# v behind the second half of the scores, and the next image's statistics beside the first scores, in an attention kernel

## The chip, the cores and the metric

The kernel runs on one NeuronCore of a Trainium2 chip. The metric is the device time of one execution in microseconds. The kernel before took 1803.81 us, the median of three runs (1803.52 to 1804.42).

## What is computed

The input x has 32 images of 32 x 32 positions with 256 channels. Each image is normalised by groups (32 groups of 8 channels, over all positions), goes through single-head self-attention over its 1024 positions, and is added to x:

```python
scale = jnp.float32(c) ** (-0.5)
x = inputs.reshape(B, H * W, c)
q = x @ Wq + bq
k = x @ Wk + bk
v = x @ Wv + bv
scores = jnp.einsum('bnc,bmc->bnm', q, k) * scale
attn = jax.nn.softmax(scores, axis=-1)
attended = jnp.einsum('bnm,bmc->bnc', attn, v)
out = attended @ Wo + bo
...
x = x + _L0_conv_ref(_gn(x), ...)
```

## The kernel before

Wq and Wk are folded into one matrix, Wv and Wo into another, so that each image needs one projection "g" (4 banks of 128 x 512), one projection "v" (4 banks), the scores of h with g, and the attend of the exponentials with v. Every float32 operand of a matmul is kept as a coarse part (`_hi`) and a rest (`_lo`), and a product is three matmuls (hi hi, hi lo, lo hi).

An image b is worked in two halves c of 512 queries. The scores of a half are 8 tiles m (128 keys x 512 queries, 6 matmuls each, `scores`, L933). They go through four PSUM banks `ps_s`; ScalarE reads each out to `s_buf[c]` (`scores_out`, L343), and TensorE may write tile m + 4 only then (semaphore `s_out`). VectorE takes the maximum over the 8 tiles (`maxima`, five steps, L584), turns and reduces it (`part_maxima`, `query_maxima`, `row_maxima`), and subtracts it in four pieces of two tiles (`difference`, L621). ScalarE makes two exponentials of each piece: the coarse `p_hi` (`exponentials_hi`, L349) and the full one in place (`exponentials`, L358); VectorE makes the rest `p_lo` (`p_rest`, L628). The attend (L946) is four tiles j of 24 matmuls into `ps_o[j]`; its first tile waits for `p_lo` piece by piece. `finish` (L636) divides by the sum of the exponentials (a column of ones in v) and adds the bias; POOL's `store` adds the result to a copy of x in the output.

The banks of g and v are shared with these: `ps_g` is `ps_o[0]`, `ps_o[1]`, `ps_s[2]`, `ps_s[3]`. ScalarE reads g and v out (`g_part`, `v_part`), VectorE makes their rests (`g_rest`, `v_rest`).

The next image is prepared beside this. SP loads x_t(b + 1) as soon as `h_rest(b)` is done. VectorE takes its statistics (`channel_stats`, `channel_sums`, `group_means`, `group_spread`, `group_variance`), POOL raises to the power -1/2 (`inverse_std`), VectorE turns the result back (`turn_back`), ScalarE shifts x_t in place (`shift`) and makes `h_hi` (`h_parts`), VectorE `h_lo` (`h_rest`), and TensorE projects g(b + 1).

Nothing schedules this: each engine has a list written out by hand, and takes its instructions in that order. TensorE's (L995) is, per image:

```python
for m in range(T):
    scores(b, 0, m)
for j in range(TQ):
    attend(b - 1, 1, j)
project_v(b, first=first)
for m in range(T):
    scores(b, 1, m, first_v=first)
for j in range(TQ):
    attend(b, 0, j)
project_g(b + 1)
```

Image 0 has lists of its own (`first_image`), the last one too (`last_image`); images 1 to 30 take `body`. In image 1 VectorE's `body(1, True)` puts the statistics behind the last `v_rest` (late_stats), in the others they stand ahead of the first.

Of the kernel before, what the change touches and what calls it, by code (L numbers as in the profile page):

```python
# [42 lines left out]
def attention_kernel(nc, x, x_turned, wq, bq, wk, bk, wv, bv, wo, bo, out):  # L43
    B, H, W, C = x.shape
    N = H * W
    T = N // P
# [6 lines left out]
    NP = T // PIECE  # L53
# [13 lines left out]
    with ExitStack() as ctx:  # L67
# [103 lines left out]
        bn_done = sem("bn_done")  # L171
# [105 lines left out]
        @block.gpsimd  # L277
        def _(pool):
            pool.memset(ident[:], 0.0).then_inc(const_step, 1)
            pool.memset(chan[:], 0.0).then_inc(const_step, 1)  # L280
            pool.memset(ones[:], 1.0).then_inc(const_step, 1)
            pool.memset(minus_half[:], -0.5).then_inc(const_step, 1)
            pool.memset(v_hi[:, :, 0:1].bitcast(F32), 1.0).then_inc(const_step, 1)
            pool.memset(v_hi[:, :, 1:VC - C].bitcast(F32), 0.0).then_inc(const_step, 1)
            pool.wait_ge(const_step, 6)
            pool.affine_select(out=ident[:], in_=ident[:], compare_op=ALU.not_equal, fill=1.0, base=0,
                               pattern=[[-1, P]], channel_multiplier=1).then_inc(const_step, 1)

            def store(b, c):

                after(pool, x_copied[c], b * 16 + 16)
                after(pool, o_out, b * 8 + (4 * c + 4))
                pool.dma_start(out_v[b, :, c * TQ:(c + 1) * TQ, :], o_buf[c][:],  # L293
                               accum_op=ALU.add).then_inc(stored[c], 16)

            def inverse_std(b):
                pool.wait_ge(var_done, b + 1)
                pool.tensor_tensor(group_stats[:, 1, :], g_var[:], minus_half[:], ALU.pow).then_inc(rstd_done, 1)  # L298

            inverse_std(0)  # L300

            inverse_std(1)
            store(0, 0)
            with pool.Fori(1, B - 1) as b:
                store(b - 1, 1)
                inverse_std(b + 1)
                store(b, 0)
            store(B - 2, 1)
            store(B - 1, 0)
# [3 lines left out]
        def _(act):  # L313
# [4 lines left out]

            def h_parts(b):
                act.wait_ge(s_ps, b * 16)  # L320
                for k in range(K):
                    act.wait_ge(h_done, b * 2 + (k + 1))
                    nc.scalar.activation(h_hi[:, k, :], x_t[:, k, :], ACT.Identity,
                                         scale=norm[:, 1, k:k + 1]).then_inc(h_hi_done, 1)
# [24 lines left out]
            def exponentials_hi(b, c, i):  # L349

                rows = slice(i * PIECE, (i + 1) * PIECE)
                if i == 0:
                    after(act, o_ps, b * 8 + (4 * c + 4 - 8))
                act.wait_ge(diff_done, b * 8 + (4 * c + i + 1))
                nc.scalar.activation(p_hi[c][:, rows, :], s_buf[c][:, rows, :], ACT.Exp,  # L355
                                     scale=SCALE).then_inc(p_hi_done, 1)
# [33 lines left out]
            act.wait_ge(fold_ps, 4)  # L390
            nc.scalar.activation(out_bias[:], ps_ob[:, 0:C], ACT.Copy).then_inc(out_bias_done, 1)

            def softmax_beside(b, c, project):

                for i in range(NP - 1):
                    exponentials_hi(b, c, i)
                    if i == 1:
                        project(2)
                    exponentials(b, c, i)
                    if i == 0:  # L400
                        project(0)
                        project(1)
                    elif i == 1:
                        project(3)

            def last_exponentials(b, c):
                exponentials_hi(b, c, NP - 1)
                exponentials(b, c, NP - 1)

            def first_image():  # L410

# [36 lines left out]
                for m in range(4, T):  # L448
                    scores_out(1, 0, m)

            def scores_first(b):

                scores_out(b, 0, 0)
                last_exponentials(b - 1, 1)
                for m in range(1, T):
                    scores_out(b, 0, m)

            def body(b):

                softmax_beside(b, 0, lambda i: v_part(b, i))  # L460
                scores_out(b, 1, 0)
                last_exponentials(b, 0)
                for m in range(1, T):
                    scores_out(b, 1, m)
                shift(b + 1, 0)
                shift(b + 1, 1)
                h_parts(b + 1)
                softmax_beside(b, 1, lambda i: g_part(b + 1, i))

            def last_image(b):  # L470

                scores_out(b, 0, 0)
                last_exponentials(b - 1, 1)
                for m in range(1, T):
                    scores_out(b, 0, m)
                scores_out(b, 1, 0)
                scores_out(b, 1, 1)
                scores_out(b, 1, 2)
                for i in range(NP):
                    exponentials_hi(b, 0, i)  # L480
                    exponentials(b, 0, i)
                    scores_out(b, 1, 3 + i)
                scores_out(b, 1, 7)
                for i in range(4):
                    v_part(b, i)
                for i in range(NP):
                    exponentials_hi(b, 1, i)
                    exponentials(b, 1, i)
# [1 line left out]
            first_image()  # L490
            body(1)
            with act.Fori(2, B - 1) as b:
                scores_first(b)
                body(b)
            last_image(B - 1)

# [2 lines left out]
        def _(dve):  # L499
# [195 lines left out]
            def first_image():  # L695
# [45 lines left out]
                p_rest(0, 1, 1)  # L741
                finish(0, 0, 3)
                p_rest(0, 1, 2)
                maxima(1, 0, 0)
                p_rest(0, 1, 3)
                for step in range(1, 5):
                    maxima(1, 0, step)

            def softmax_beside(b, c, finish_tile, h_next, project, next_stats, next_sums, late_stats=False):

                part_maxima(b, c)
                finish_tile(0)
                h_next(0)
                h_next(1)
                query_maxima(b, c)
                finish_tile(1)
                row_maxima(b, c)
                difference(b, c, 0)
                difference(b, c, 1)
                finish_tile(2)  # L760
                difference(b, c, 2)
                if not late_stats:
                    next_stats()
                project(0)
                if not late_stats:
                    next_sums()
                finish_tile(3)
                project(1)
                p_rest(b, c, 0)
                project(2)  # L770
                difference(b, c, 3)
                project(3)
                if late_stats:
                    next_stats()
                p_rest(b, c, 1)
                if late_stats:
                    next_sums()
                p_rest(b, c, 2)
                p_rest(b, c, 3)

            def scores_first(b):

                for step in range(5):
                    maxima(b, 0, step)

            def body(b, late_stats=False):
                def next_stats():
                    channel_stats(b + 1)
                    dve.wait_ge(bn_done, b * 4 + 8)

                softmax_beside(b, 0, lambda j: finish(b - 1, 1, j), nothing, lambda i: v_rest(b, i),
                               next_stats, lambda: channel_sums(b + 1), late_stats)
                group_means(b + 1)
                group_spread(b + 1)
                maxima(b, 1, 0)
                group_variance(b + 1)
                maxima(b, 1, 1)
                maxima(b, 1, 2)
                turn_back(b + 1)
                maxima(b, 1, 3)  # L800
                maxima(b, 1, 4)
                softmax_beside(b, 1, lambda j: finish(b, 0, j), lambda k: h_rest(b + 1, k),
                               lambda i: g_rest(b + 1, i), nothing, nothing)

            def last_image(b):

# [40 lines left out]
                                        ALU.add).then_inc(x_last_done, 1)  # L847

            first_image()
            body(1, True)  # L850
            with dve.Fori(2, B - 1) as b:
                scores_first(b)
                body(b)
# [7 lines left out]
        def _(pe):  # L861
# [52 lines left out]
                    product(ps_g[i][:], [(a[:, kk, rows], h[:, kk, cols]) for kk in range(K)  # L914
                                             for a, h in ((a_hi, h_hi), (a_hi, h_lo), (a_lo, h_hi))], g_ps)

            def project_v(b, scores_done=8, first=False):

                for i in FIRST_V if first else range(4):
                    if first and i >= 2:  # L920
# [74 lines left out]
            def body(b, first=False):  # L995
                for m in range(T):
                    scores(b, 0, m)
                if not first:
                    for j in range(TQ):
                        attend(b - 1, 1, j)  # L1000
                project_v(b, first=first)
                for m in range(T):
                    scores(b, 1, m, first_v=first)
                for j in range(TQ):
                    attend(b, 0, j)
                project_g(b + 1)

            def last_image(b):
# [47 lines left out]
```

## Time and profile before

| | |
|---|---|
| median of 3 runs | 1803.81 us (1803.52 to 1804.42) |
| the profiled execution, its own time | 1804.24 us |
| its span in the profile | 1802.6 us |
| granted TensorE clock | 1.00 throughout |
| TensorE busy | 1796.6 us (100%) |
| VectorE busy | 1638.7 us (91%) |
| ScalarE busy | 1056.1 us (59%) |
| GpSimd (POOL) busy | 91.1 us (5%) |

Times in the timelines are microseconds from the start of the span; the execution's own time is 1.6 us more than the span. Matmuls are pipelined and overlap in the records, each lasting 0.28 or 0.39 us while they follow one another more closely, so the length of a stage is read from start to start. A row of a timeline that ends in x2 or x4 is a run of like instructions, and its length that of the whole run.

### The profile page before, as it was taken

The page shows a single profiled execution, that of the slowest core. Times are in us where ns is not written, and L with a number is a line of the kernel's source. Part 1 is how long each engine was busy: PE and PEld are TensorE (multiplying, and loading weights), DVE is VectorE, ACT ScalarE, POOL GpSimd, SP SyncE. Part 2 cuts the span into 40 slices and gives each one's busy share as a digit, 9 for nine tenths or more (in the row PEclk, how much of TensorE's full clock was granted, in tenths as well). Part 3 has the DMA queues.
Part 4 walks back from the last instruction along what each step waited for, and adds up shares of the span by engine and source line. Part 5 has one row for each costly group of instructions (what it writes and reads, how often), then busy time and mean ns, then how long its engine had stood idle before and what let it go on. Part 6 is the DMA issues. An engine that isn't in the chain of part 4 may idle for free.

```text
span 1802.6 us, 32710 instructions
## 1 busy us (share of the span) xinstructions
PE 1796.6 (100%) x11589; PEld 1643.1 (91%) x11589; DVE 1638.7 (91%) x2860; ACT 1056.1 (59%) x1417; POOL 91.1 (5%) x106
## 2 busy tenths in 40 slices
PE   9999999999999999999999999999999999999999
PEld 8989999899899999998999989999899898999989
DVE  7999899999999999989999999899998999999997
ACT  5565565665655656556565565565665656656563
POOL 0000000000000000000000000000000000000000
PEclk9999999999999999999999999999999999999999
DMA  3222122321222221213212222122321222311201
GB/s 117 59 71 69 26 57 58 70 70 37 44 60 68 70 54 27 70 58 70 58 23 70 58 70 65 23 64 58 70 70 36 46 60 68 70 48 33 67 14 36
DMA packets 28809, 101.92 MB, mean 57 GB/s; under 512 B 3189, under 2 KB 3962, under 8 KB 28794
## 3 DMA queue, kind: packets, MB, share of 16 engines
q0 software_dynamic: 9072, 33.03, 12.1%
q1 hardware_dynamic: 19722, 68.69, 11.7%
q8 instruction: 9, 0.15, 0.0%
q14 instruction: 6, 0.05, 0.0%
HBM read 68.16 MB, written 66.58 MB: 75 GB/s over the span
## 4 chain that ended last, share of the span: by engine, by line
PE 97%; DVE 2%; issue 1%; POOL 0%; ACT 0%; POOLq 0%; DVEq 0%; ACTq 0%
PE ps_s L865 48%; PE ps_o L959 13%; PE ps_o L960 13%; PE ps_o L961 13%; PE ps_o L865 10%; DVE s_buf L625 0%; PE ps_o L969 0%; DVE top L595 0%; DVE o_buf L645 0%; DVE h_lo L567 0%; DVE query_max L612 0%; POOL group_stats L298 0%; DVE top_turned L600 0%; DVE g_lo L575 0%; DVE part_max L602 0%
## 5 line engine op out<-in xcount | busy, mean ns | idle before, releaser
L959 PE MATMUL ps_o<-v_rows,p_hi 128*128 128x258 f32 x2048 | 577.9, 282 | 0.0
L961 PE MATMUL ps_o<-v_rows,p_lo 128*128 128x258 f32 x2048 | 576.1, 281 | 0.0
L960 PE MATMUL ps_o<-v_lo,p_hi 128*128 128x256 f32 x2048 | 575.8, 281 | 0.0
L355 ACT ACTIVATE p_hi<-s_buf 128x1024 fp32r<-128x1024 f32 x256 | 272.3, 1063 | 417.6 <-DVE s_buf L625 417.6
L865 PE MATMUL ps_s<-g_hi,h_hi 128*128 128x512 f32 x1024 | 399.2, 390 | 0.4 <-DVE g_lo L575 0.3
L865 PE MATMUL ps_s<-g_hi,h_lo 128*128 128x512 f32 x1024 | 399.0, 390 | 0.0
L865 PE MATMUL ps_s<-g_lo,h_hi 128*128 128x512 f32 x1024 | 398.6, 389 | 0.0
L959 PEld LDWEIGHTS ps_o<-v_rows,p_hi 128*128 128x128 f32 x2048 | 385.9, 188 | 2.4
L960 PEld LDWEIGHTS ps_o<-v_lo,p_hi 128*128 128x128 f32 x2048 | 384.8, 188 | 2.9
L347 ACT ACTIVATE s_buf<-ps_s 128x512 f32<-128x512 f32 x512 | 293.1, 607 | 160.4 <-PE ps_s L865 158.7
L961 PEld LDWEIGHTS ps_o<-v_rows,p_lo 128*128 128x128 f32 x2048 | 384.5, 188 | 0.0
L633 DVE TENSOR_TENSOR p_lo<-s_buf,p_hi 128x1024 fp32r<-128x1024 f32 x256 | 306.9, 1219 | 39.1 <-ACT s_buf L361 39.1
L625 DVE TENSOR_TENSOR s_buf<-s_buf,row_max 128x1024 f32<-128x1024 f32 x256 | 306.7, 1219 | 2.1
L361 ACT ACTIVATE s_buf<-s_buf 128x1024 f32<-128x1024 f32 x256 | 271.3, 1060 | 0.0
L865 PEld LDWEIGHTS ps_s<-g_hi,h_hi 128*128 128x128 f32 x1024 | 192.2, 188 | 40.4 <-issue 0.8
L865 PEld LDWEIGHTS ps_s<-g_hi,h_lo 128*128 128x128 f32 x1024 | 192.2, 188 | 40.3
L865 PEld LDWEIGHTS ps_s<-g_lo,h_hi 128*128 128x128 f32 x1024 | 192.2, 188 | 38.8
L595 DVE TENSOR_TENSOR top<-top,s_buf 128x512 f32<-128x512 f32 (+1 forms) x192 | 167.3, 871 | 40.1 <-ACT s_buf L347 25.0
L645 DVE SCALAR_TENSOR_TENSOR o_buf<-ps_o,rden,out_bias 128x256 f32<-128x256 f32 x252 | 121.9, 484 | 14.5
L293 POOL DMA_DIRECT2D out_dram<-o_buf x63 | 56.1, 891 | 1397.5 <-DVE o_buf L645 1380.2
L340 ACT ACTIVATE v_rows<-ps_o 128x512 fp32r<-128x512 f32 x64 | 38.3, 599 | 105.9 <-PE ps_o L865 105.8
L595 DVE TENSOR_TENSOR top<-s_buf 128x1024 f32<-128x1024 f32 x64 | 78.2, 1222 | 7.7 <-ACT s_buf L347 7.7
(95 smaller groups left out, 2229.6 us busy)
## 6 DMA issues: line engine op xcount, KB each, us to landing
x_t<-in_x_turned_dram SPq DMA_DIRECT2D x64, 512.0 KB, 4.0
out_dram<-in_x_dram SPq DMA_DIRECT2D x63, 512.0 KB, 7.1
out_dram<-o_buf POOLq DMA_DIRECT2D x63, 512.0 KB, 5.4
x_last<-in_x_dram SPq DMA_DIRECT2D x1, 512.0 KB, 7.8
out_dram<-o_buf SPq DMA_DIRECT2D x4, 128.0 KB, 1.9
s_buf<-in_L_conv_Wq_dram SPq DMA_DIRECT2D x1, 256.0 KB, 4.6
s_buf<-in_L_conv_Wk_dram SPq DMA_DIRECT2D x1, 256.0 KB, 5.0
s_buf<-in_L_conv_Wv_dram SPq DMA_DIRECT2D x1, 256.0 KB, 5.2
```

The costliest lines, as they stand in the source:

```text
L293: pool.dma_start(out_v[b, :, c * TQ:(c + 1) * TQ, :], o_buf[c][:], accum_op=ALU.add).then_inc(stored[c], 16)
L347: nc.scalar.activation(s_buf[c][:, m, :], ps_s[(8 * c + m) % SB][:], ACT.Copy).then_inc(s_out, 1)
L355: nc.scalar.activation(p_hi[c][:, rows, :], s_buf[c][:, rows, :], ACT.Exp, scale=SCALE).then_inc(p_hi_done, 1)
L361: nc.scalar.activation(piece, piece, ACT.Exp, scale=SCALE).then_inc(p_done, 1)
L595: nc.vector.tensor_tensor(to, left, right, ALU.max).then_inc(top_step, 1)
L625: nc.vector.tensor_tensor(piece, piece, row_max[:].unsqueeze(1).broadcast_to([P, PIECE, Q]), ALU.subtract).then_inc(diff_done, 1)
L633: nc.vector.tensor_tensor(p_lo[c][:, rows, :], s_buf[c][:, rows, :], p_hi[c][:, rows, :].bitcast(F32), ALU.subtract).then_inc(p_lo_done, 1)
L645: nc.vector.scalar_tensor_tensor(out=o_buf[c][:, j, :], in0=ps_o[j][:, VC - C:VC], scalar=rden[:, t:t + 1], in1=out_bias[:] if rows is Non ...
L865: last = nc.tensor.matmul(ps, stationary, moving, start=start and n == 0, stop=stop and n == len(pairs) - 1)
L959: nc.tensor.matmul(ps[:, 0:VC], p_hi[c][:, m, cols], v_hi[:, m, :], start=m == 0, stop=False)
L960: nc.tensor.matmul(ps[:, VC - C:VC], p_hi[c][:, m, cols], v_lo[:, m, :], start=False, stop=False)
L961: last = nc.tensor.matmul(ps[:, 0:VC], p_lo[c][:, m, cols], v_hi[:, m, :], start=False, stop=m == T - 1)
```

## The change

TensorE takes `project_v(b)` behind the second half of the scores, right ahead of `attend(b, 0)`. The scores of the second half no longer wait for `v_lo`; v's third bank waits for the readout of all 16 score tiles instead of 8; `attend(b, 0)` waits for `v_lo` by piece in its first tile. Image 0 keeps the old order. ScalarE and VectorE get new lists for the body to match, for image 1 too (no late_stats), and the last pair of exponentials of c = 1 is done within the image. VectorE's statistics of image b + 1 stand beside the maxima of the first scores of b. POOL takes `inverse_std(b + 1)` ahead of `store(b - 1, 1)`.

```diff
             with pool.Fori(1, B - 1) as b:
+                inverse_std(b + 1)
                 store(b - 1, 1)
-                inverse_std(b + 1)
                 store(b, 0)
...
             def h_parts(b):
                 act.wait_ge(s_ps, b * 16)
+                act.wait_ge(v_ps, b * 4)
                 for k in range(K):
...
+            def pair(b, c, i):
+                exponentials_hi(b, c, i)
+                exponentials(b, c, i)
...
             def body(b):
                 shift(b + 1, 0)
                 shift(b + 1, 1)
+                pair(b, 0, 0)
+                pair(b, 0, 1)
+                scores_out(b, 1, 0)
+                pair(b, 0, 2)
+                scores_out(b, 1, 1)
+                scores_out(b, 1, 2)
+                exponentials_hi(b, 0, 3)
+                scores_out(b, 1, 3)
+                exponentials(b, 0, 3)
+                for m in range(4, T):
+                    scores_out(b, 1, m)
+                for i in range(4):
+                    v_part(b, i)
                 h_parts(b + 1)
+                pair(b, 1, 0)
+                pair(b, 1, 1)
+                g_part(b + 1, 0)
+                exponentials_hi(b, 1, 2)
+                g_part(b + 1, 1)
+                exponentials(b, 1, 2)
+                g_part(b + 1, 2)
+                exponentials_hi(b, 1, 3)
+                g_part(b + 1, 3)
+                exponentials(b, 1, 3)
             def last_image(b):
+                for m in range(T):
                     scores_out(b, 0, m)
                 scores_out(b, 1, 0)
                 scores_out(b, 1, 1)
...
             first_image()
             body(1)
             with act.Fori(2, B - 1) as b:
-                scores_first(b)
+                for m in range(T):
+                    scores_out(b, 0, m)
                 body(b)
             last_image(B - 1)
...
                 p_rest(0, 1, 1)
                 finish(0, 0, 3)
                 p_rest(0, 1, 2)
                 p_rest(0, 1, 3)
+                scores_first(1)
             def scores_first(b):
+                channel_stats(b + 1)
+                dve.wait_ge(bn_done, b * 4 + 8)
+                maxima(b, 0, 0)
+                channel_sums(b + 1)
+                maxima(b, 0, 1)
                 group_means(b + 1)
                 group_spread(b + 1)
+                maxima(b, 0, 2)
                 group_variance(b + 1)
+                maxima(b, 0, 3)
+                maxima(b, 0, 4)
+            def body(b):
+                part_maxima(b, 0)
                 turn_back(b + 1)
+                finish(b - 1, 1, 0)
+                query_maxima(b, 0)
+                finish(b - 1, 1, 1)
+                row_maxima(b, 0)
+                difference(b, 0, 0)
+                difference(b, 0, 1)
+                finish(b - 1, 1, 2)
+                difference(b, 0, 2)
+                difference(b, 0, 3)
+                finish(b - 1, 1, 3)
+                for i in range(NP):
+                    p_rest(b, 0, i)
+                for step in range(5):
+                    maxima(b, 1, step)
+                v_rest(b, 0)
+                part_maxima(b, 1)
+                for i in (1, 2, 3):
+                    v_rest(b, i)
+                query_maxima(b, 1)
+                row_maxima(b, 1)
+                h_rest(b + 1, 0)
+                h_rest(b + 1, 1)
+                finish(b, 0, 0)
+                difference(b, 1, 0)
+                difference(b, 1, 1)
+                finish(b, 0, 1)
+                difference(b, 1, 2)
+                difference(b, 1, 3)
+                finish(b, 0, 2)
+                finish(b, 0, 3)
+                g_rest(b + 1, 0)
+                g_rest(b + 1, 1)
+                p_rest(b, 1, 0)
+                g_rest(b + 1, 2)
+                p_rest(b, 1, 1)
+                g_rest(b + 1, 3)
+                p_rest(b, 1, 2)
+                p_rest(b, 1, 3)
             def last_image(b):
...
                                         ALU.add).then_inc(x_last_done, 1)
             first_image()
-            body(1, True)
+            body(1)
             with dve.Fori(2, B - 1) as b:
                 scores_first(b)
                 body(b)
...
                     product(ps_g[i][:], [(a[:, kk, rows], h[:, kk, cols]) for kk in range(K)
                                              for a, h in ((a_hi, h_hi), (a_hi, h_lo), (a_lo, h_hi))], g_ps)
-            def project_v(b, scores_done=8, first=False):
+            def project_v(b, scores_done=16, first=False):
                 for i in FIRST_V if first else range(4):
                     if first and i >= 2:
...
                 if not first:
                     for j in range(TQ):
                         attend(b - 1, 1, j)
-                project_v(b, first=first)
-                for m in range(T):
-                    scores(b, 1, m, first_v=first)
+                if first:
+                    project_v(b, first=True)
+                    for m in range(T):
+                        scores(b, 1, m, first_v=True)
+                else:
+                    for m in range(T):
+                        scores(b, 1, m, True)
+                    project_v(b, 16)
                 for j in range(TQ):
-                    attend(b, 0, j)
+                    attend(b, 0, j, not first)
                 project_g(b + 1)
             def last_image(b):
```

The new lists are shown with "+"; the old ones that they replace stand in the listing above. Below, the rows of three places as they stand on the engine (line, operation, tiles, shape). The changed kernel's lines are three lower on VectorE and one higher on most of ScalarE's.

VectorE, from the third `p_rest` of image 0 on (`p_lo` is written by `p_rest`, `top` by `maxima`, `top_turned` by `part_maxima`), before:

```order
L633 TENSOR_TENSOR p_lo<-s_buf,p_hi 128x1024
L595 TENSOR_TENSOR top<-s_buf 128x1024
L633 TENSOR_TENSOR p_lo<-s_buf,p_hi 128x1024
L595 TENSOR_TENSOR top<-top,s_buf 128x1024
L595 TENSOR_TENSOR top<-top 128x512
L595 TENSOR_TENSOR top<-top,s_buf 128x512 x2
L600 STREAM_TRANSPOSE top_turned<-top 128x512
L602 TENSOR_REDUCE part_max<-top_turned 128x16
L640 RECIPROCAL rden<-ps_o 128x1
L645 SCALAR_TENSOR_TENSOR o_buf<-ps_o,rden,out_bias 128x256
L609 COPY parts<-part_max 32x16 x4
```

And in the changed kernel:

```order
L630 TENSOR_TENSOR p_lo<-s_buf,p_hi 128x1024 x2
L502 BN_STATS bn_parts<-x_t 128x6 x4
L592 TENSOR_TENSOR top<-s_buf 128x1024
L508 BN_AGGR chan<-bn_parts 128x2 x2
L592 TENSOR_TENSOR top<-top,s_buf 128x1024
L519 STREAM_TRANSPOSE chan_turned<-chan 128x64
L522 TENSOR_REDUCE mean_sum<-chan_turned 128x4
L527 SCALAR_TENSOR_TENSOR dev<-mean_sum,chan_turned 128x32
L530 TENSOR_SCALAR group_stats<-mean_sum 128x4
L533 TENSOR_TENSOR dev<-dev 128x32
L535 TENSOR_TENSOR spread<-chan_turned,dev 128x32
L592 TENSOR_TENSOR top<-top 128x512
```

The statistics of image 2, from `bn_parts` to `spread`, have come in ahead of the maxima and between them, and the last `p_rest` of image 0 stands ahead of all of them.

ScalarE, in image 1 from the end of the first half's readouts on (`s_buf<-ps_s` is a readout of a score, `v_rows` one of v, `p_hi<-s_buf` and `s_buf<-s_buf` are the two exponentials of a piece), before:

```order
L355 ACTIVATE p_hi<-s_buf 128x1024
L361 ACTIVATE s_buf<-s_buf 128x1024
L340 ACTIVATE v_rows<-ps_o 128x2x256 x2
L355 ACTIVATE p_hi<-s_buf 128x1024
L340 ACTIVATE v_rows<-ps_s 128x2x256
L361 ACTIVATE s_buf<-s_buf 128x1024
L340 ACTIVATE v_rows<-ps_s 128x2x256
L355 ACTIVATE p_hi<-s_buf 128x1024
L361 ACTIVATE s_buf<-s_buf 128x1024
L347 ACTIVATE s_buf<-ps_s 128x512
L355 ACTIVATE p_hi<-s_buf 128x1024
L361 ACTIVATE s_buf<-s_buf 128x1024
```

And in the changed kernel:

```order
L317 ACTIVATE x_t<-x_t,norm 128x1024 x2
L356 ACTIVATE p_hi<-s_buf 128x1024
L362 ACTIVATE s_buf<-s_buf 128x1024
L356 ACTIVATE p_hi<-s_buf 128x1024
L362 ACTIVATE s_buf<-s_buf 128x1024
L348 ACTIVATE s_buf<-ps_s 128x512
L356 ACTIVATE p_hi<-s_buf 128x1024
L362 ACTIVATE s_buf<-s_buf 128x1024
L348 ACTIVATE s_buf<-ps_s 128x512 x2
L356 ACTIVATE p_hi<-s_buf 128x1024
L348 ACTIVATE s_buf<-ps_s 128x512
L362 ACTIVATE s_buf<-s_buf 128x1024
```

The shift (`x_t`) leads, the readouts of v have left the exponentials, and the first readout of the second half stands behind four exponentials instead of six and the four of v.

VectorE, in image 1 from the first `p_rest` of the first half on, before:

```order
L633 TENSOR_TENSOR p_lo<-s_buf,p_hi 128x1024
L581 TENSOR_TENSOR v_lo<-ps_s,v_rows 128x512
L625 TENSOR_TENSOR s_buf<-s_buf,row_max 128x1024
L581 TENSOR_TENSOR v_lo<-ps_s,v_rows 128x512
L505 BN_STATS bn_parts<-x_t 128x6 x4
L633 TENSOR_TENSOR p_lo<-s_buf,p_hi 128x1024
L511 BN_AGGR chan<-bn_parts 128x2 x2
L633 TENSOR_TENSOR p_lo<-s_buf,p_hi 128x1024 x2
```

And in the changed kernel:

```order
L630 TENSOR_TENSOR p_lo<-s_buf,p_hi 128x1024 x4
L592 TENSOR_TENSOR top<-s_buf 128x1024
L592 TENSOR_TENSOR top<-top,s_buf 128x1024
L592 TENSOR_TENSOR top<-top 128x512
L592 TENSOR_TENSOR top<-top,s_buf 128x512 x2
L578 TENSOR_TENSOR v_lo<-ps_o,v_rows 128x512
L597 STREAM_TRANSPOSE top_turned<-top 128x512
L599 TENSOR_REDUCE part_max<-top_turned 128x16
L578 TENSOR_TENSOR v_lo<-ps_o,v_rows 128x512
L578 TENSOR_TENSOR v_lo<-ps_s,v_rows 128x512 x2
L606 COPY parts<-part_max 32x16 x4
```

`v_rest` (`v_lo`) has moved from between the `p_rest` to behind the maxima of the second half, the first one ahead of the transpose and reduction, the other three behind them.

## Rows read from the trace of the kernel before

**Rows 1.** The page's busy times by engine, over the whole span
```profile
PE 1796.6 (100%) x11589; PEld 1643.1 (91%) x11589; DVE 1638.7 (91%) x2860; ACT 1056.1 (59%) x1417; POOL 91.1 (5%) x106
```

**Rows 2.** The page's costly groups: first matmuls of a score (busy, mean, idle before)
```profile
L865 PE MATMUL ps_s<-g_hi,h_hi 128*128 128x512 f32 x1024 | 399.2, 390 | 0.4 <-DVE g_lo L575 0.3
```

**Rows 3.** Timeline of TensorE, image 16: start us, length, engine, line, instruction
```profile
901.44 0.39 PE L865 MATMUL ps_s<-g_hi,h_hi 128*128 128x512 f32 x1
...
923.76 0.28 PE L865 MATMUL ps_o<-vo_hi,h_hi 128*128 128x256 f32 x1
...
929.36 0.40 PE L865 MATMUL ps_s<-g_hi,h_hi 128*128 128x512 f32 x1
...
940.27 0.28 PE L959 MATMUL ps_o<-v_rows,p_hi 128*128 128x258 f32 x1
...
957.16 0.39 PE L865 MATMUL ps_s<-g_hi,h_hi 128*128 128x512 f32 x1
```

**Rows 4.** Timeline of ScalarE, image 1 (idle before it in brackets)
```profile
86.78 1.06 ACT L355 ACTIVATE p_hi<-s_buf 128x1024 fp32r<-128x1024 f32 x1 [10.05 <-DVE s_buf L625]
...
94.60 1.06 ACT L361 ACTIVATE s_buf<-s_buf 128x1024 f32<-128x1024 f32 x1
95.55 0.60 ACT L347 ACTIVATE s_buf<-ps_s 128x512 f32<-128x512 f32 x1
96.03 1.08 ACT L355 ACTIVATE p_hi<-s_buf 128x1024 fp32r<-128x1024 f32 x1
```

**Rows 5.** The page's DMA issues (KB each, us from issue to landing)
```profile
x_t<-in_x_turned_dram SPq DMA_DIRECT2D x64, 512.0 KB, 4.0
```

**Rows 6.** Timeline of VectorE, image 1
```profile
85.46 2.36 DVE L625 TENSOR_TENSOR s_buf<-s_buf,row_max 128x1024 f32<-128x1024 f32 x2
...
94.42 0.68 DVE L581 TENSOR_TENSOR v_lo<-ps_s,v_rows 128x512 fp32r<-128x512 f32 x1
95.02 2.46 DVE L505 BATCH_NORM_STATS2 bn_parts<-x_t 128x6 f32<-128x512 f32 x4
...
98.66 0.28 DVE L511 BATCH_NORM_AGGREGATE chan<-bn_parts 128x2 f32<-128x12 f32 x2
98.85 2.31 DVE L633 TENSOR_TENSOR p_lo<-s_buf,p_hi 128x1024 fp32r<-128x1024 f32 x2
101.08 0.24 DVE L522 STREAM_TRANSPOSE chan_turned<-chan 128x64 f32<-128x64 f32 x1
...
102.13 1.22 DVE L595 TENSOR_TENSOR top<-s_buf 128x1024 f32<-128x1024 f32 x1
103.26 0.18 DVE L543 TENSOR_REDUCE var_sum<-spread 128x4 f32<-128x32 f32 x1
...
103.56 1.23 DVE L595 TENSOR_TENSOR top<-top,s_buf 128x1024 f32<-128x1024 f32 x1
...
105.78 0.24 DVE L550 STREAM_TRANSPOSE norm<-group_stats 128x64 f32<-128x64 f32 x1 [0.27 <-POOL group_stats L298]
105.95 1.38 DVE L595 TENSOR_TENSOR top<-top,s_buf 128x512 f32<-128x512 f32 x2
107.36 0.71 DVE L600 STREAM_TRANSPOSE top_turned<-top 128x512 f32<-128x512 f32 x1
...
108.72 0.16 DVE L640 RECIPROCAL rden<-ps_o 128x1 f32<-128x1 f32 x1
```

**Rows 7.** Timeline of TensorE, image 1, first matmul of v
```profile
87.31 0.28 PE L865 MATMUL ps_o<-vo_hi,h_hi 128*128 128x256 f32 x1
```

**Rows 8.** Timeline of TensorE, from image 1 to image 2
```profile
120.48 0.39 PE L865 MATMUL ps_s<-h_hi,a_lo 128*128 128x512 f32 x1
121.22 0.49 PE L865 MATMUL ps_s<-g_hi,h_hi 128*128 128x512 f32 x1 [0.35 <-DVE g_lo L575]
121.55 0.40 PE L865 MATMUL ps_s<-g_lo,h_hi 128*128 128x512 f32 x1
```

**Rows 9.** Windows: length, busy (x), granted clock, DMA share, GB/s, first microseconds
```profile
2.00:8.00 6.00, 5.99 (x32) 5.99 (x33) 3.44 (x10) 0.15 (x1) 0.00 (x0) 1.00 0.96 343
```

More of the change, by code:

```diff
@@ L391, in _ @@
             nc.scalar.activation(out_bias[:], ps_ob[:, 0:C], ACT.Copy).then_inc(out_bias_done, 1)
[L393 to L408, printed above, removed]
+            def pair(b, c, i):
+                exponentials_hi(b, c, i)
+                exponentials(b, c, i)
             def first_image():
@@ L449, in first_image @@
                     scores_out(1, 0, m)
[L451 to L456, printed above, removed]
-            def body(b):
[L460 to L464, printed above, removed]
+            def body(b):
                 shift(b + 1, 0)
                 shift(b + 1, 1)
-                h_parts(b + 1)
-                softmax_beside(b, 1, lambda i: g_part(b + 1, i))
+                pair(b, 0, 0)
[11 more added lines that the diff above has]
+                    v_part(b, i)
+                h_parts(b + 1)
+                pair(b, 1, 0)
[8 more added lines that the diff above has]
+                exponentials(b, 1, 3)
             def last_image(b):
-                scores_out(b, 0, 0)
-                last_exponentials(b - 1, 1)
-                for m in range(1, T):
+                for m in range(T):
                     scores_out(b, 0, m)
@@ L743, in first_image @@
                 p_rest(0, 1, 2)
-                maxima(1, 0, 0)
                 p_rest(0, 1, 3)
[L746 to L779, printed above, removed]
@@ L781, in scores_first @@
-            def scores_first(b):
[L783 to L792, printed above, removed]
+                scores_first(1)
@@ L793, in body @@
+            def scores_first(b):
+                channel_stats(b + 1)
[3 more added lines that the diff above has]
+                maxima(b, 0, 1)
                 group_means(b + 1)
                 group_spread(b + 1)
-                maxima(b, 1, 0)
+                maxima(b, 0, 2)
                 group_variance(b + 1)
-                maxima(b, 1, 1)
-                maxima(b, 1, 2)
+                maxima(b, 0, 3)
+                maxima(b, 0, 4)
@@ L799, in body @@
+            def body(b):
+                part_maxima(b, 0)
                 turn_back(b + 1)
[L800 to L803, printed above, removed]
+                finish(b - 1, 1, 0)
[36 more added lines that the diff above has]
+                p_rest(b, 1, 3)
```

## Prediction

> **What bounds the kernel now.** I read the busy times first, then TensorE's waits, then the timeline of a middle image, then that of image 1, since the change handles image 1 like the rest where the old code had an exception for it. TensorE is busy throughout and VectorE 91% [rows 1]; the 1024 first matmuls of the score groups lost 0.4 us in all to waits [rows 2]. The middle image [rows 3] has no hole: first half of the scores, attend of the image before (c=1), v, second half of the scores, attend (c=0), projection of g. The starts give the stage lengths: v 929.36 - 923.76 = 5.60, a half of the scores 940.27 - 929.36 = 10.91, so an attend 923.76 - 901.44 - 10.91 = 11.41, g 957.16 - 940.27 - 11.41 = 5.48, the image 957.16 - 901.44 = 55.72 us. The 32 images at that pace are 1783 of 1802.6 us; the rest is set-up and the tail. So the same matmuls cannot go faster than they go. **An edit of the order can win only the few tenths that TensorE waits, and can lose where it makes TensorE wait.** The sum is a count of new holes on TensorE.
>
> **The change part by part.** No instruction is added or removed but for waits. I give times from the start of an image's first score ("t"); ScalarE's and VectorE's steps are start-to-start intervals.
>
> *TensorE.* Second half of the scores now starts at 10.91 + 11.41 = 22.32, where v stood, v at 33.23, attend c=0 at 38.83 as before. Sum of the stages: unchanged. The scores lose their wait on v_lo; v's third bank waits for the readout of the last score; the first tile of attend waits for v_lo by piece, 0.72 us apart (a tile is 11.41 / 4 = 2.85, a piece a quarter of it).
>
> *ScalarE and VectorE in a middle image.* ScalarE now puts the four readouts of g between the last two pairs of exponentials instead of carrying the last pair into the next image. The first g bank is ready at -5.48 + 1.37 + 0.2 = -3.9; four more exponentials at 0.95 (95.55 - 94.60 [rows 4]) and three readouts, by my estimate 0.57 each, put the last exponential's end at about 2.3. VectorE follows with p_rest 2 and 3 and begins the statistics of the next image at about 4.9. What stands between there and the first difference is priced on image 1 next; carried over, the first readout of the second half ends at about 25.0, while TensorE needs it for the fifth score at 22.32 + 5.46 = 27.8: 2.8 spare. The last exponential of c=0 ends at 30.2; then p_rest 1.12, five maxima 4.75, v_rest 0 to 36.7, transpose and reduction 1.36, v_rest 1 to 38.7, needed at 38.83 + 0.72 = 39.55: 0.85 spare. v_rest 3 hangs on TensorE's own pace: v ends 38.83, readout from 39.05 to 39.65, v_rest to 40.35, needed at 41.0: 0.65 spare, the thinnest joint, and VectorE idles some tenths ahead of it. h_lo is done at about 45.3, needed at 50.2. g_lo 1 is done some 0.8 ahead of the next image's first score. **So the middle images cost nothing: 0.**
>
> *Moved statistics and the queues.* The load of x_t is issued when h_lo is done, at t of about 45, and lands 4.0 us later [rows 5]; the statistics, which used to read it half an image later, now read it some 15 us behind the issue. Still covered; if the cover were gone, VectorE would wait there with the maxima behind it and TensorE behind those. On POOL the inverse deviation now stands ahead of the store of the image before; its input is ready at t of about 12, the store's not before 24, so the store is not delayed. The shift on ScalarE (two steps of about 1.1) falls into the wait ahead of the first exponential, 10 us long in image 1 [rows 4]. h_hi now waits for v too, which ends at 38.83, as the readouts ahead of it do. Each of these: 0.
>
> *Image 1.* It comes from first_image, whose order is the old one, so here the lead is missing. In the trace the first difference of image 1 starts at 85.46 [rows 6]. Ahead of it the change now puts the statistics of image 2, which the old code had (late_stats) behind the v_rests: bn_stats 2.46; channel sums 98.85 - 98.66 = 0.19; group means and spread 102.13 - 101.08 = 1.05; variance 103.56 - 103.26 = 0.30; turn_back 105.95 - 105.78 = 0.17; together 4.17 [rows 6]. Difference 0 starts at 89.63. The second half of the scores starts where v did, at 87.31 [rows 7], 5.60 us earlier than it did: **4.2 us later meets 5.6 us earlier.** In steps:
> - ScalarE starts the first exponential 86.78 - 85.46 = 1.32 behind difference 0 [rows 4, 6]: 90.95. The readout of score 0 stands behind four exponentials, 0.95 each: 94.75, ends after 0.60 at 95.35.
> - TensorE wants its bank for the fifth score at 87.31 + 5.46 = 92.77. Hole of 2.58, 0.05 for the signal.
> - Readout 1 stands behind one more readout and two exponentials: 94.75 + 0.48 (96.03 - 95.55 [rows 4]) + 1.90 = 97.13, ends 97.73. TensorE, due at 95.40 + 0.10 + 1.36 = 96.86, waits to 97.78. (0.10: the first matmul behind a wait takes 0.33 to the next where 0.23 is usual [rows 8].) Readouts 2 and 3 end at 98.2 and 99.6, the latter needed at 100.6. Lost so far: 97.78 - (87.31 + 6.82) = 3.65, with the resumption 3.75.
> - The last exponential runs 99.52 to 100.58; p_rest 3 1.12 (half of 101.08 - 98.85); the maxima 107.36 - 102.13 = 5.23, less 0.30, 0.17 and a wait of 0.27 between them, and some 0.25 more where those steps had filled gaps, 4.75; v_rest 0 0.60 (95.02 - 94.42); transpose and reduction 108.72 - 107.36 = 1.36; v_rest 1 ends 0.68 on, at 109.1 [rows 6]. TensorE ends the scores at 87.31 + 10.91 + 3.75 = 101.97 and wants it at 101.97 + 5.60 + 0.72 = 108.3: 0.8, and 0.1.
> - Statistics now fill gaps between maxima that depend on each other, 0.1 to 0.2 back. Sum about 4.6.
>
> *Given back.* In the old order image 2 opens with a hole: 121.22 - 120.48 = 0.74 between matmuls that are 0.227 apart, and 0.10 behind it [rows 8], since late_stats delayed g_lo. Now g_lo 1 comes some 0.9 before it is needed: -0.6.
>
> **Sum:** 4.6 - 0.6 = +4.0 us on the profiled execution's own 1804.24, which is 0.43 above the median; on the median 1803.81 + 4.0 = **1807.8**. The steps' errors are tenths, those of two medians too: 1807.2 to 1808.6. A measurement of this kernel tells about 0.2%, 3.6 us, from no change; 4.0 is just above.
>
> **Rivals.**
> *A. Not slower: image 1 hides the lateness.* The old ScalarE waited 10 us at this very place [rows 4], and TensorE lost nothing. The deciding point is the readout of score 0: if it ends before 92.77, both score holes go, the later v hole with them (its chain starts with the same exponentials), and the old 0.6 goes too: 1803.81 - 0.6 = 1803.2. For it speaks that wait; against it, that v's 5.60 us lay between it and the scores. 8%.
> *B. Holes in every middle image.* If VectorE is late by over 0.65 to 0.85 us at the v_rests, each further tenth costs 29 x 0.1 = 2.9 us. For it: VectorE has 9% idle and the chain readout, exponential, p_lo, maxima, v_lo stands in one row. At 0.3 us an image: 1807.8 + 8.7 = 1816.5. Against it: the durations repeat within hundredths, and the wait ahead of v_rest 3 is a cushion. 10%.
> *C. The clock falls.* The granted clock was 1.00 in the 6 us behind the first 2 us without a matmul [rows 9]; the new longest hole is 2.6 us, longer than any the trace shows inside the work. If the clock fell to 1.2 GHz for one stage of scores, that costs between nothing and 10.91 again: up to 1818.7. I take nothing, the value of the nearest row. 4%. The Trainium skill (TensorE: Matmul & The Clock Gate, Part 1) says that the array's default is the half rate and that an idle array returns to it. By that rule the pause would be punished twice; the row of this trace doesn't show it.
> *D. Nothing of it bites, or something is gained beyond the 0.6:* 2%; TensorE leaves no room for it.
>
> **How the numbers follow.** Forecast 76%, A 8%, B 10%, C 4%, D 2%. The forecast lies 0.4 above the bound of 3.6 us with an error of that size, so about 7 in 10 of it is slower by over 0.2% and the rest within: slower 0.54 + 0.10 + 0.04 = 0.68; within 0.22 + 0.08 = 0.30; faster 0.02. The range runs from 1805.5 to 1811.5: the forecast with twice its errors, and the mild end of B (0.1 us an image). A and most of B and C, under 2 in 10, stay out.
>
> **What would show it.** In the new profile: TensorE's period in the middle images still 55.72 with no hole; in image 1 two waits for the readouts of scores 0 and 1 of 2.5 and 0.9 us, and one of 0.8 on v_lo in the first attend tile; no wait at the start of image 2; ScalarE's last exponential before the image's first readout; clock 1.00. Wrong would be a period over 55.8, a hole on g_lo or at attend's fourth piece in each image, or image 1 without holes.

## The result, and the profile after

The changed kernel takes 1806.96 us (median of 20 runs, 1806.20 to 1807.77), the kernel before 1804.01 (20 runs). The ratio is 1.0016, 95% interval 1.0010 to 1.0022: 2.95 us more. The forecast was +4.0 and 1807.8. The profiled execution took 1807.02 us, with a span of 1805.3 (before 1802.6).

The page of the changed kernel: busy times, the chain that ended last, and the two groups of TensorE that waited (those of before are [rows 1, 2]).

```profile
PE 1796.1 (99%) x11589; PEld 1641.9 (91%) x11589; DVE 1627.7 (90%) x2860; ACT 1070.1 (59%) x1417; POOL 104.8 (6%) x106
...
PE 95%; DVE 3%; ACT 1%; issue 0%; DMA 0%; SPq 0%; DVEq 0%; ACTq 0%
...
L956 PE MATMUL ps_o<-v_rows,p_hi 128*128 128x258 f32 x2048 | 577.7, 282 | 0.6 <-DVE v_lo L578 0.6
...
L862 PE MATMUL ps_s<-g_hi,h_hi 128*128 128x512 f32 x1024 | 399.2, 390 | 3.1 <-ACT s_buf L348 3.0
```

TensorE did the same work and waited 3.1 us at scores and 0.6 at the attend. The timeline of TensorE shows where: nearly all of it is in image 1 (start us, length, engine, line, instruction).

```profile
87.19 0.40 PE L862 MATMUL ps_s<-g_hi,h_hi 128*128 128x512 f32 x1
...
92.42 0.39 PE L862 MATMUL ps_s<-g_hi,h_lo 128*128 128x512 f32 x1
95.11 0.50 PE L862 MATMUL ps_s<-g_hi,h_hi 128*128 128x512 f32 x1 [2.31 <-ACT s_buf L348]
...
96.38 0.39 PE L862 MATMUL ps_s<-g_hi,h_lo 128*128 128x512 f32 x1
97.50 0.50 PE L862 MATMUL ps_s<-g_hi,h_hi 128*128 128x512 f32 x1 [0.73 <-ACT s_buf L348]
...
101.72 0.28 PE L862 MATMUL ps_o<-vo_hi,h_hi 128*128 128x256 f32 x1
...
107.33 0.28 PE L956 MATMUL ps_o<-v_rows,p_hi 128*128 128x258 f32 x1
...
108.83 0.36 PE L956 MATMUL ps_o<-v_rows,p_hi 128*128 128x258 f32 x1 [0.62 <-DVE v_lo L578]
...
119.62 0.40 PE L862 MATMUL ps_o<-h_hi,a_hi 128*128 128x512 f32 x1
...
125.07 0.39 PE L862 MATMUL ps_s<-g_hi,h_hi 128*128 128x512 f32 x1
```

The second scores took 101.72 - 87.19 = 14.53 us (10.91 before), the attend of the first half ("first attend" below) 119.62 - 107.33 = 12.29 (11.44 before). The idle times in brackets are counted from the modelled end of the matmul ahead. From start to start the three matmuls came 95.11 - 92.42 - 0.23 = 2.46, 0.89 and 0.79 us late. Behind them image 2 starts without a wait, where it had lost 0.6 [rows 8]. The releasers in image 1, first the timeline of ScalarE, then that of VectorE:

```profile
90.68 1.06 ACT L356 ACTIVATE p_hi<-s_buf 128x1024 fp32r<-128x1024 f32 x1 [2.93 <-DVE s_buf L622]
...
94.48 0.58 ACT L348 ACTIVATE s_buf<-ps_s 128x512 f32<-128x512 f32 x1
```

```profile
89.36 2.36 DVE L622 TENSOR_TENSOR s_buf<-s_buf,row_max 128x1024 f32<-128x1024 f32 x2
...
108.00 0.68 DVE L578 TENSOR_TENSOR v_lo<-ps_o,v_rows 128x512 fp32r<-128x512 f32 x1
```

Difference 0 at 89.36 (forecast 89.63), the first exponential at 90.68 (90.95), readout 0 at 94.48 (94.75), v_rest 1 ended at 108.68 (109.1).

The middle images have no wait. In image 16 of the changed kernel, its first score, its difference 0 and its v_rest 1 (timelines of TensorE and VectorE):

```profile
904.68 0.39 PE L862 MATMUL ps_s<-g_hi,h_hi 128*128 128x512 f32 x1
...
923.90 2.36 DVE L622 TENSOR_TENSOR s_buf<-s_buf,row_max 128x1024 f32<-128x1024 f32 x2
...
942.75 0.68 DVE L578 TENSOR_TENSOR v_lo<-ps_o,v_rows 128x512 fp32r<-128x512 f32 x1
```

Difference 0 starts 19.22 us behind the first score there, and 89.36 - 64.87 = 24.49 in image 1: 5.3 later. v_rest 1 ends at 38.75, 0.8 ahead of its need. The first score of image 3 and of image 31 from TensorE's timeline, first in the changed kernel, then in the one before:

```profile
180.76 0.39 PE L862 MATMUL ps_s<-g_hi,h_hi 128*128 128x512 f32 x1
...
1739.98 0.39 PE L862 MATMUL ps_s<-g_hi,h_hi 128*128 128x512 f32 x1
```

```profile
177.08 0.39 PE L865 MATMUL ps_s<-g_hi,h_hi 128*128 128x512 f32 x1
...
1737.24 0.39 PE L865 MATMUL ps_s<-g_hi,h_hi 128*128 128x512 f32 x1
```

28 images take 1559.22 us after and 1560.16 before, 55.686 and 55.720 each: the new order is 0.034 us shorter per image, which the prediction does not have.

### The profile page after: what moved, and what is told of

Read it like the earlier page. It is cut to its first block, busy times and chain, and to the rows that moved or that the text cites. A ratio compares the mean times of both kernels' runs of the same rounds, so it can differ in the third digit from the quotient of the medians.

```text
span 1805.3 us, 32859 instructions
## 1 busy us (share of the span) xinstructions
PE 1796.1 (99%) x11589; PEld 1641.9 (91%) x11589; DVE 1627.7 (90%) x2860; ACT 1070.1 (59%) x1417; POOL 104.8 (6%) x106
## 4 chain that ended last, share of the span: by engine, by line
PE 95%; DVE 3%; ACT 1%; issue 0%; DMA 0%; SPq 0%; DVEq 0%; ACTq 0%
PE ps_s L862 46%; PE ps_o L956 13%; PE ps_o L957 13%; PE ps_o L958 13%; PE ps_o L862 9%; DVE top L592 1%; ACT p_hi L356 0%; ACT s_buf L362 0%; DVE s_buf L622 0%; DMA s_buf<-in_L_conv_Wq_dram 0%; DVE p_lo L630 0%; ACT s_buf L348 0%; DVE o_buf L642 0%; DVE query_max L609 0%; DVE top_turned L597 0%
## 5 line engine op out<-in xcount | busy, mean ns | idle before, releaser
L348 ACT ACTIVATE s_buf<-ps_s 128x512 f32<-128x512 f32 x512 | 301.6, 598 | 196.1 <-PE ps_s L862 190.2
L622 DVE TENSOR_TENSOR s_buf<-s_buf,row_max 128x1024 f32<-128x1024 f32 x256 | 301.6, 1219 | 1.1
L317 ACT ACTIVATE x_t<-x_t,norm 128x1024 f32<-128x1024 f32 x62 | 68.0, 1145 | 117.1 <-DVE norm L547 117.1
```

The lines of the kernel that those rows point to most:

```text
L317: nc.scalar.activation(x_t[:, k, :], x_t[:, k, :], ACT.Identity, bias=norm[:, 0, k:k + 1]).then_inc(h_done, 1)
L348: nc.scalar.activation(s_buf[c][:, m, :], ps_s[(8 * c + m) % SB][:], ACT.Copy).then_inc(s_out, 1)
L622: nc.vector.tensor_tensor(piece, piece, row_max[:].unsqueeze(1).broadcast_to([P, PIECE, Q]), ALU.subtract).then_inc(diff_done, 1)
```

## Experiments

The theory: TensorE's holes are made where VectorE enters the new lists, in image 1, 5.3 us later than in a middle image; elsewhere the order is free. I compare spans of image 1, from its first score to image 2's: before 121.22 - 64.99 = 56.23 us, after 125.07 - 64.87 = 60.20. (Its own start varies by 1.2 us, 64.26 to 65.44, between kernels whose TensorE list is the same up to there, and the whole span varies with it. Runs 2, 3, 4 and 6 are one execution each.)

**1. The old lists in image 1.**

```diff
-            body(1)
+            old_body(1)
+            body(2)
```

`old_body` is the loop body of the kernel before, on TensorE, ScalarE and VectorE; POOL's store of image 0 goes back ahead of the inverse deviation of image 2, and the loops of the new order begin at image 2 or 3.

> All four engines take the old lists in image 1 and the new ones from image 2 on; nothing is left out. Lead theory (TensorE's holes come only from image 1, where VectorE enters the new list some 5.7 us later than in a middle image): the stage of the second scores and the first attend of image 1 go back to 10.9 and 11.4 us, which gives back 3.6 + 0.9 = 4.5; the old hole at the start of image 2 (0.6) returns, and the handover leaves VectorE some 2 us late in image 2, worth one hole of about 1.2 at v_lo there. Span 1802.6 to 1803.0, time about 1804.3. Rival 1 (the new order costs in the middle images and image 1 is incidental): time stays at 1807. Rival 2 (the handover only moves the lateness whole into image 2): again 3.5 to 4.5 of holes, in image 2, time 1806.5 to 1807.5.

Measured 1804.67 us (11 runs; before 1804.25; ratio 1.0002, 0.9993 to 1.0011). Image 1 took 56.23, the old 0.6 is back at image 2, and one hole stands in image 2's first attend (12.56 instead of 11.42). TensorE's waits on v_lo and g_lo in this kernel (total, times, longest):

```profile
PE ps_o L1042 <- DVE v_lo L611: 0.9, 1, 0.9
PE ps_s L948 <- DVE g_lo L605: 0.3, 1, 0.3
```

The lead theory holds: the loss was image 1's, 60.20 - 56.23 = 3.97 us, and of its lateness 1.14 came back in image 2, not the whole.

**2. Fewer statistics in image 1.**

```diff
+            def few_stats(b):
...
+                    nc.vector.bn_stats(bn_parts[:, k, h, :], x_t[:, k, h * Q:h * Q + 16]).then_inc(bn_done, 1)
...
-                scores_first(1)
+                scores_first(1, few_stats)
```

> The changed kernel, but the statistics of image 2 alone are taken over 16 instead of 512 columns per instruction (four bn_stats on VectorE in image 1), so image 2's normalisation is of a sample: work is left out. Lead theory: these instructions shrink from 2.46 to about 0.4 us, everything behind them on VectorE and ScalarE comes 2.0 earlier, the second scores of image 1 take 12.5 instead of 14.53 us, the first attend stays at 12.3 since both the v_rest and TensorE come earlier by the same, span 1803.3. Rival (the holes are made by the order on ScalarE, four exponentials ahead of the first readout, whenever they start, or by the shift ahead of them): both stages stay as they are, span 1805.3.

One run: 1804.29 us, span 1802.6 (1803.3 expected; image 1 began 0.6 earlier than in the changed kernel). The second scores took 12.45 us, the first attend 12.27; image 1 took 58.10, 2.1 less than in the changed kernel. TensorE's waits on engines in this kernel:

```profile
PE ps_s L869 <- ACT s_buf L348: 1.0, 2, 0.7
PE ps_o L963 <- DVE v_lo L585: 0.6, 1, 0.6
```

The hole at the scores shrank by 14.53 - 12.45 = 2.08 us when VectorE had some 2 us less to do ahead of its first difference: it is VectorE's lateness. The wait on v_lo stayed at 0.6.

**3. The statistics alone, v where it was.**

```diff
             def scores_first(b):
+                channel_stats(b + 1)
...
+                maxima(b, 0, 0)
+                channel_sums(b + 1)
...
-            body(1, True)
+            body(1)
```

> The kernel before with one part of the change: the statistics of the next image stand beside the first scores' maxima, in image 1 too; v stays ahead of the second scores, and shift, turn_back and POOL stay where they were. Lead theory: middle images have no hole, period 55.72, since v's 5.6 us still lie between the first half and the readouts of the second. In image 1 the first difference comes 4.1 late; holes of about 1.6 at v_lo in the third score and up to 0.5 more, 2.0 in all, the old 0.6 at image 2 stays or shrinks: span 1804.0 to 1804.8. Rival (the early statistics by themselves cause all of the loss): span 1805.3 or more with 4.5 us of holes in image 1.

One run: 1804.74 us, span 1803.1 (1804.0 to 1804.8 expected; image 1 began 0.7 earlier than in the kernel before). Image 1 took 57.58, 1.35 more than before. TensorE lost 1.86 us in it where 2.0 were expected: 1.36 at v_lo in the third score, the rest at a readout behind it and in v; and no hole is left at image 2. Middle images: (1737.74 - 177.59) / 28 = 55.72. So the early statistics alone cause less than half of image 1's holes. TensorE's wait on v_lo there:

```profile
PE ps_s L869 <- DVE v_lo L581: 1.1, 1, 1.1
```

**4. v alone, the statistics where they were.**

```diff
-                channel_stats(b + 1)
...
                 difference(b, 0, 2)
+                channel_stats(b + 1)
...
                 difference(b, 0, 3)
```

> The changed kernel with the statistics back where the old lists had them (bn_stats behind the third difference, the small steps beside the second half's maxima, the shift ahead of h_hi), v moved as in the change. Lead theory: image 1 has no hole at the scores, but now every image is late at v_lo: the statistics lie between the first difference and v_rest, 2.5 + 1.9 us with an idle of 1.8 to fill, so v_rest 1 ends some 0.9 behind the second piece's due time, 1.0 with the resumption. Period 56.7, 30 images: time 1830 to 1840. Rival (the statistics' place does not matter in the middle images, only v's does): period 55.69, time about 1803 to 1804.

One run: 1830.49 us, span 1828.8. Images 2 to 30 have one hole each, at the second piece of the first attend (12.26 to 12.28 us instead of 11.42), and images 3 to 30 take 56.53 each (56.7 expected). Image 1 has two, of 1.34 us at the first piece and 1.04 at the second, and takes 58.59, more than in the kernel before; but its scores have no hole (10.89). TensorE's waits on v_lo (total, times, longest):

```profile
PE ps_o L958 <- DVE v_lo L578: 19.8, 31, 1.3
```

31 waits, 0.64 on the mean. A wait of 0.60 lengthens the attend by some 0.85: the idle time is counted from a modelled end, 0.16 behind the next start that would be due, and the first matmul behind it takes 0.08 longer to the next. **The two moves need each other**: v right ahead of the attend costs 26 us by itself, and what makes it free is that the statistics leave the stretch between the first difference and v_rest.

**5. All v_rest ahead of the reduction, in image 1.**

```diff
                 v_rest(b, 0)
-                part_maxima(b, 1)
+                if not v_first:
+                    part_maxima(b, 1)
                 for i in (1, 2, 3):
                     v_rest(b, i)
+                if v_first:
+                    part_maxima(b, 1)
...
-            body(1)
+            body(1, True)
```

> The changed kernel, but in image 1 alone VectorE makes all four v_rest ahead of the transpose and reduction of the second half's maxima. Lead theory with the joint at v_rest 1 as read: the first attend of image 1 goes from 12.29 to 11.43 us, the second scores stay at 14.53, nothing opens behind it; span 1804.4, time about 1806.1. Rival (VectorE's lateness is conserved and the hole only moves): the 0.9 comes back at g_lo ahead of image 2 or at the projection of g, time 1807.0.

Measured 1806.62 us (10 runs; before 1804.22; ratio 1.0015, 1.0006 to 1.0024), span 1804.9. The attend went to 11.42 as expected, and nothing opened behind it, but the scores took 15.10 instead of 14.53. TensorE's matmuls were nearly twice as far apart behind the hole (0.43 us instead of 0.23), and the windows show why. First the timeline of TensorE in this kernel, then its windows (stretch, length, busy of PE, PEld, DVE, ACT, POOL, then the granted clock, DMA share, GB/s):

```profile
94.94 0.57 PE L865 MATMUL ps_s<-g_hi,h_hi 128*128 128x512 f32 x1 [2.30 <-ACT s_buf L348]
...
96.17 0.63 PE L865 MATMUL ps_s<-g_hi,h_hi 128*128 128x512 f32 x1
96.59 0.63 PE L865 MATMUL ps_s<-g_lo,h_hi 128*128 128x512 f32 x1
```

```profile
94.00:95.00 1.00, 0.06 (x1) 0.06 (x1) 0.96 (x4) 1.00 (x3) 0.00 (x0) 1.00 0.00 0
95.00:98.70 3.70, 3.70 (x9) 2.72 (x10) 3.42 (x4) 3.70 (x6) 0.92 (x1) 0.54 0.44 40
98.70:100.00 1.30, 1.30 (x7) 1.08 (x6) 0.00 (x0) 1.30 (x2) 0.00 (x0) 1.00 1.07 211
```

The granted clock fell to 1.2 GHz behind 2.3 us without a matmul. It cost 0.57, not the whole 1.7 of nine matmuls 0.2 further apart, since the second hole (0.89 from start to start, and 0.10 behind it) was eaten by it. This edit is not what made it fall: the order up to there is the changed kernel's, whose profiled execution had the same pause of 2.31 us and a clock of 1.00 behind it. The mean clock was 0.999 in all 10 runs of this kernel. The time, 1806.62, is 0.5 above the one expected, about what the fall cost.

**6. Readouts ahead of the exponentials, in image 1.**

```diff
+                    scores_out(b, 1, 0)
+                    pair(b, 0, 0)
+                    scores_out(b, 1, 1)
+                    exponentials_hi(b, 0, 1)
+                    scores_out(b, 1, 2)
...
```

> The changed kernel, but in image 1 alone ScalarE reads out score 0 of the second half ahead of the first exponential, and scores 1 to 3 one exponential or two apart behind it, so all four banks are free before TensorE wants them (92.65, 94.0, 95.4, 96.7). Conserved-lateness theory (VectorE enters image 1 late; the readouts only decide where TensorE meets it): the second scores go from 14.53 to 10.9 us, but the last exponential ends only 0.5 earlier, so v_rest 1 is 0.5 earlier where TensorE is 3.6 earlier: the first attend goes from 12.29 to 15.4, and the span stays at 1805 (1804.6 to 1805.4). Rival (the readouts behind four exponentials are the cause, the v hole is a separate small one): second scores 10.9, attend 12.3 or less, span 1801.7.

One run: 1807.56 us, span 1805.9. The second scores took 10.89, and the hole moved and split in three: 0.76 us idle ahead of v's third bank, which now waits for the last readout, then 1.42 ahead of the attend's first piece and 1.04 ahead of its second, both on v_lo. From start to start v took 8.20 (5.60), the wait for the first piece included, and the attend 14.35. v_rest 1 ended 43.30 us behind the image's start, 0.5 before the 43.81 of the changed kernel, as expected. Image 1 took 61.22; the clock had fallen again, though no pause was over 1.42 us, as a window of its first attend shows (columns as above):

```profile
108.20:111.60 3.40, 3.40 (x18) 3.40 (x17) 3.14 (x12) 0.00 (x0) 0.00 (x0) 0.51 0.02 5
```

In 3.40 us at 0.51 some 1.7 us of work are lost; without that image 1 would be near 59.5 by my estimate, 0.7 below the 60.20 of the changed kernel. So the readouts mostly decide where TensorE meets VectorE's lateness. The expectation put all of it into the attend and had neither v's stage nor the clock.

**7 and 8. Old lists in image 1, and v_rest ahead of the reduction in image 2.**

```diff
+            old_body(1, True)
+            scores_first(2)
+            body(2, True)
```

In both, image 1 keeps the old lists, and image 2 on VectorE has its four `v_rest` ahead of `part_maxima` (`body(2, True)`). Run 8 alone adds in VectorE's image 1, second half, one `finish_tile` set behind `project(1)`:

```diff
+                if c == 1:
+                    project(1)
+                    finish_tile(3)
```

> The old lists in image 1 on all engines, the new ones from image 2 on, and in image 2 alone the four v_rest ahead of the transpose and reduction. Theory: the hole of 1.14 us that stood in the first attend of image 2 (12.56) goes, the old 0.6 at the start of image 2 stays, and the 29 images of 55.69 instead of 55.72 us give 0.8: span 1801.2, time about 1803.5, 0.5 to 0.8 below the kernel before. Rival (VectorE is still too late and the hole comes back at g_lo of image 3): time 1804.3 to 1804.7.

> As the run before, and in image 1 (the old list) VectorE makes the second g_rest ahead of the last finish. Theory: g_lo 1 is ready some 0.6 earlier, at or ahead of the end of the projection of g, and the last hole, 0.6 at the start of image 2, goes: span 1800.6, time about 1802.9, 1.1 below the kernel before. Rival (the finish that now comes later holds up a bank): the hole moves to the attend of image 2, time as the run before.

Run 7: 1803.32 us (11 runs; before 1804.22, 27 runs; ratio 0.9997, 0.9988 to 1.0006). Run 8: 1803.23 (11 runs; 0.9994, 0.9985 to 1.0003), span 1801.4 for both. In both image 2's first attend takes 11.42. In run 8 image 2 starts without a wait (image 1 takes 55.72), but 0.3 comes back in its two halves of scores, 0.2 of it at a readout. From image 1's first score to the end the profiled executions are 0.98 and 1.31 us shorter than the kernel before: 29 x 0.034 = 0.99, and in run 8 another 0.3 to 0.4 of the hole of 0.65. The medians lie 0.9 and 1.0 below the kernel before; the intervals reach past 1, so the gain is likely, not shown, and run 8 is not shown to be better than run 7 (span 1800.6 was expected). Against the changed kernel the span is 1805.3 - 1801.4 = 3.9 us shorter.

## Why the prediction was right

- *The bound* was right in kind: the loss is a count of holes, and the matmuls kept their pace. That the sum of the stages stays unchanged was off by hundredths, see below.
- *Image 1* was right in mechanism, place and nearly in size: scores 3.62 lost (forecast 3.75), attend 0.85 (0.9), each of VectorE's and ScalarE's times 0.27 to 0.4 early, 0.12 of that because this execution reached image 1 so much earlier. Together 4.47, where the forecast's terms, 4.65 less 0.1 to 0.2, add up to 4.5 and not to the 4.6 that it carries on. Runs 1 and 2 show the cause.
- *Given back*: 0.65 at image 2 (0.6).
- *The middle images cost 0*: right about the holes, and about the joints. v_rest 1 ends 38.75 us behind the first score (forecast 38.7) and v_rest 3 at 40.34 (40.35), each 0.6 to 0.8 ahead of its need. Run 4 shows how near the rival of holes in every image (B) lay, had the statistics stayed.
- *The term that was mis-sized* is the stages' sum, called unchanged: they are 0.034 us shorter, 28 times, 0.95 us. With it the forecast would have been 3.0 to 3.1, and the measured is 2.95. The forecast measured one half of the scores, the one behind v, and took the attend and g from it by subtraction; but a half behind g or behind an attend takes 10.89, behind v 10.91, and an attend takes 11.43 to 11.44 behind scores, 11.42 behind v. So the difference comes with TensorE's order: kernels with v ahead of the second scores (before, run 3) have 55.72, all others without middle holes (after, runs 1, 2, 5 to 8) 55.69. Why, no run here tells. Because of this term the median, 1806.96, lies below the 1807.2 to 1808.6 that the forecast gives for errors of tenths, and inside its range.
- *Rival A* (the wait of ScalarE hides it) fell: the hole is there, and run 2 ties it to VectorE's arrival.
- *Rival C* (the clock falls), at 4%, was put too low in chance and far too high in price. The changed kernel's mean granted clock was 0.999 in 14 of 20 runs and 1.000 in 6, the profiled one among these. The means are 1807.05 and 1806.79 us; the 0.3 between them is less than the scatter within each group (0.4), so the runs do not show a price. Run 5 does: 0.57 in its scores. The nearest row [rows 9] was no fair guide: it lies at the program's start, not in dense work. The rule of the Trainium skill (TensorE: Matmul & The Clock Gate, Part 1), that an idle array returns to the half rate, agrees with run 5, where the clock fell behind an idle array. It does not tell the profiled execution of the changed kernel, which kept 1.00 behind the same pause, from the 14 runs that did not.
- *The bound of 3.6 us*: the result, 0.16%, is within it, the side to which the forecast gives 0.30 against 0.68 for slower by more.

## What to carry to other kernels

Where lists are written by hand, price the change where the loop is entered, not only in its steady image: an order that needs a lead of several microseconds may have none in the first one. Moving the instruction that waits (here a readout) moves the hole; moving work off the late engine removes it. When TensorE has no idle time left, count new holes, and read every stage's length for itself and to hundredths, for thirty repeats make them a microsecond.

## What the runs showed of the hardware

- Behind a single pause of 2.3 us in otherwise dense matmuls the granted clock fell to 0.54 over the next 3.70 us in run 5; in the changed kernel's profiled execution it stayed at 1.00 behind the same pause, while the mean was below 1 in 14 of its 20 runs (which pause it was, those do not tell).
- Three shorter pauses within 7 us, 0.76, 1.42 and 1.04 us, were followed by 0.51 over 3.40 us in run 6. Two such pauses alone, 1.34 and 1.04 us in image 1 of run 4, were not, nor its 29 single pauses of 0.6: its clock was 1.00. The old kernel's waits are at most 0.4 us inside the work, and its clock was 1.00 in every run that lists it.
- The first matmul of 512 columns behind a wait is followed after 0.32 to 0.35 us, otherwise 0.227; in the attend it is 0.19 to 0.23 instead of 0.12. So a hole costs about 0.1 more than the time by which the matmul comes late.
